# An FFN behind a LoRA projection: scaled f16 parts and seven block products for the base projection of batches 2 and 3

## The reference

```python
base   = x @ W.T                                  # W 1024 x 1024, f32
logits = x @ Wr.T + 5 * onehot(language)          # 8 experts, top 2, softmax -> gates
h_a    = x @ A.T                                  # 8 experts x rank 16 = 128 columns
c      = base + 2 * sum_e gates[e] * (h_a[e] @ B[e].T)
out    = x + (silu(c @ Wg.T) * (c @ Wu.T)) @ Wd.T  # Wg, Wu 3584 x 1024, Wd 1024 x 3584, f16
```

## Time and profile before

| | |
|---|---|
| median of 3 runs | 1346.72 us |
| time of the profiled execution | 1346.81 us |
| its span, first to last instruction | 1345.0 us |
| TensorE clock granted | 1.000 of full speed |
| gate/up of batch 1, of batch 2 | 410.0 to 589.6, 740.0 to 920.1 us of the span |
| route and base of batch 2, of batch 3 | 589.6 to 646.7, 920.2 to 977.2 us |

### The profile page before, as it was taken

The page is one execution under the profiler, slowest core; times in us unless marked ns, Lnnn a source line. Parts: engine busy times, 40 slices in busy tenths (PEclk is TensorE's granted clock), DMA queues, the critical chain, the costliest instruction groups (busy, mean ns, idle before and its releaser), DMA issues.

```text
span 1345.0 us, 20793 instructions
## 1 busy us (share of the span) xinstructions
PE 1339.0 (100%) x8204; PEld 885.9 (66%) x8204; DVE 723.8 (54%) x1335; ACT 387.4 (29%) x626; POOL 173.3 (13%) x159
## 2 busy tenths in 40 slices
PE   9999999999999999999999999999999999999999
PEld 7854444486667666678667666667866766666666
DVE  6478897689524554541542555544173345555612
ACT  4366744352102333322010223332220122222100
POOL 3200112030000132213000113221200011111000
PEclk9999999999999999999999999999999999999999
DMA  7177986225954766502694567650288466666574
GB/s 254 44 262 281 371 294 240 104 98 200 339 181 143 248 215 200 179 27 91 218 332 155 187 218 234 185 161 32 75 277 289 155 178 183 181 189 195 182 231 140
DMA packets 101904, 261.19 MB, mean 194 GB/s; under 512 B 11568, under 2 KB 12208, under 8 KB 101296
## 3 DMA queue, kind: packets, MB, share of 16 engines
q1 hardware_dynamic: 101376, 259.70, 57.6%
q10 hardware_dynamic: 432, 0.17, 0.0%
HBM read 223.91 MB, written 35.91 MB: 193 GB/s over the span
## 4 chain that ended last, share of the span: by engine, by line
PE 97%; DVE 2%; DMA 1%; SPq 0%; issue 0%; ACT 0%; DVEq 0%; ACTq 0%
PE banks L624 22%; PE banks L588 19%; PE banks L645 13%; PE banks L652 13%; PE banks L581 7%; PE banks L580 7%; PE banks L500 4%; PE banks L502 4%; PE banks L501 4%; PE banks L453 1%; DVE h L891 1%; PE banks L676 1%; PE banks L456 1%; DMA a_raw<-AT 0%; PE banks L529 0%; PE banks L527 0%
## 5 line engine op out<-in xcount | busy, mean ns | idle before, releaser
L624 PE MATMUL banks<-y_hi,gu_ring 128*128 128x512 f16 x1344 | 316.5, 379 | 0.0
L624 PEld LDWEIGHTS banks<-y_hi,gu_ring 128*128 128x128 f16 x1344 | 131.5, 98 | 124.0
L645 PE MATMUL banks<-h,piece 128*128 128x512 f16 x840 | 188.5, 379 | 0.0
L580 PE MATMUL banks<-y_hi,gu_ring 128*128 128x512 f16 x432 | 163.7, 379 | 0.0
L581 PE MATMUL banks<-y_lo,gu_ring 128*128 128x512 f16 x432 | 163.7, 379 | 0.0
L1223 ACT ACTIVATE sg<-banks,sc 128x512 f32<-128x512 f32 x112 | 76.7, 686 | 241.1 <-DVE banks L999 131.9
L645 PEld LDWEIGHTS banks<-h,piece 128*128 128x128 f16 x840 | 82.2, 98 | 89.7
L1374 POOL TENSOR_TENSOR m<-m,m 128x256 f32<-128x256 f32 x84 | 61.0, 726 | 528.8 <-DVE m L980 528.8
L1002 DVE TENSOR_TENSOR banks<-banks,m 128x256 f32<-128x256 f32 x84 | 36.4, 433 | 143.7 <-PE banks L624 143.7
L1356 POOL TENSOR_TENSOR w_lo<-w_raw,w_hi 128x1024 fp32r<-128x1024 f32 x31 | 74.9, 2419 | 257.9 <-ACT w_hi L1142 250.0
L652 PE MATMUL banks<-h,piece 128*128 128x256 f16 x896 | 106.1, 273 | 0.0
(11 more groups left out here) (151 smaller groups left out, 1817.4 us busy)
## 6 DMA issues: line engine op xcount, KB each, us to landing
piece<-down_dram SPq DMA_DIRECT2D x80, 448.0 KB, 5.7
mix_c<-mix_dram SPq DMA_DIRECT2D x84, 384.0 KB, 3.9
gu_ring<-Wg SPq DMA_DIRECT2D x112, 256.0 KB, 3.0
gu_ring<-Wu SPq DMA_DIRECT2D x112, 256.0 KB, 2.9
piece<-Wd SPq DMA_DIRECT2D x64, 448.0 KB, 5.7
mix_a<-mix_dram SPq DMA_DIRECT2D x84, 256.0 KB, 2.7
mix_dram<-mixed SPq DMA_DIRECT2D x28, 640.0 KB, 3.8
w_raw<-W SPq DMA_DIRECT2D x32, 512.0 KB, 3.8
```

Source lines behind the costliest of these rows:

```text
L580: MM(bank, w[:, k, :], y_hi[:, k, :], start=(k == 0), stop=False)
L624: mm = MM(bank, w[:, k, :], y_hi[:, k, :], start=False, stop=(k == KC - 1), skip_group_check=True)
L645: mm = MM(bank, w[:, k, :], h[:, half * MH + k, 0, :], start=(start and k == 0), stop=False, skip_group_check=True)
```

## The change

Batches 0 and 1 compute their base as before. For batches 2 and 3:

- x, W, A and Wr are multiplied by a power of two each, from their largest value, and split into an f16 high and an f16 low part. High x high stays 64 matmuls of 512 columns. The two cross products (low x high and high x low), stacked along k, are one product of 2 x 2 blocks, done by seven block products in place of eight: 56 matmuls of 256 columns for a pair of chunks, 224 in a batch. Routing is the same 64 matmuls with f16 operands. LoRA and the transpose stay in f32.
- W's parts and its five block sums are made once, in steps 5 to 25 of batch 1's gate/up, for four pairs of chunks, and written to DRAM (`w16_dram`). For each batch they are loaded back in eight pieces of 256 KB a pair. W's largest value is taken in batch 0's base (`w_max`, eight reductions of 128 x 1024).
- x's largest value, parts and block sums are made on VectorE and ScalarE in steps 7 to 25 of gate/up(1) and gate/up(2). GpSimd makes no more low parts of x and W for these batches.
- In the base each pair of chunks gets the additions of the seven products: two copies on ScalarE, three additions on VectorE, one on GpSimd, and two joins on VectorE (`join`), which write half a chunk of `y_raw` while ScalarE copies the other half. `join(7)` stands behind `h_sums`. `copy_down` of the first pair waits for all eight joins.

The core of the diff (line 1 of a hunk says whose stream it is):

```diff
 # TensorE
+            def fine_route(c, ks):
...
+                for k in ks:
+                    pe.wait_ge(s_xlo, KC * c + k + 1)
+                    for t in range(TT):
+                        at = slice(t * P, (t + 1) * P)
+                        MM(banks[:, t, 0:2 * RC], x16[:, 1, k, at], ar16[:, k].rearrange("p a c -> p (a c)"),
+                           start=(k == 0), stop=False, skip_group_check=True)
+                        mm = MM(banks[:, t, 0:RC], x16[:, 0, k, at], ar16[:, k, 0], start=False,
+                                stop=(k == KC - 1), skip_group_check=True)
...
+            def fine_block(bank, second, w, x, first):
+                at = slice(HALF, T) if second else slice(0, HALF)
+                for a in range(2):
+                    for k in range(KC // 2):
+                        mm = MM(bank[:, at], w[a][:, k, :], x[:, a, k, :], start=(first and a == 0 and k == 0),
+                                stop=False, skip_group_check=True)
...
+            def fine_34(c, p):
+                pe.wait_ge(d_wb[p % 2][1], 48 * wb_loads(c, p))
+                pe.wait_ge(s_bcopy, 2 * (pair_of(c, p) + 1))
...
+            def fine_576(c, p):
+                pe.wait_ge(d_wb[p % 2][2], 48 * wb_loads(c, p))
+                pe.wait_ge(s_bs34, pair_of(c, p) + 1)
...
+            def fine_base(c):
+                fine_route(c, range(0, KC - 2))
+                fine_12(c, 0)
+                fine_route(c, range(KC - 2, KC))
+                fine_34(c, 0)
+                fine_12(c, 1)
+                fine_576(c, 0)
+                fine_34(c, 1)
+                fine_high(c, 0, 0)
+                fine_high(c, 0, 1)
+                fine_576(c, 1)
...
+                fine_576(c, 3)
+                fine_high(c, 3, 0)
+                lora(c, 6)
+                fine_high(c, 3, 1)
+                lora(c, 7)
 # VectorE
+            def w_max(o):
...
+                V.tensor_reduce(w_part[:, o:o + 1], w_hi[:, i, 0].bitcast(F32), AX.XY, ALU.max,
+                                apply_absolute_value=True).then_inc(s_wmx, 1)
...
+            def w_parts(s):
+                if s in W_LOW:
+                    p, row = W_LOW[s]
...
+                    V.scalar_tensor_tensor(out=wp[:, 1, row], in0=wp_raw[:, row], scalar=w_sc[:, 2:3], in1=wp[:, 0, row],
+                                           op0=ALU.mult, op1=ALU.subtract).then_inc(s_wpl, 1)
+                for p, c in W_SUM.get(s, ()):
...
+                    V.tensor_tensor(wp_sum[:, n % 4], left, right, op).then_inc(s_wpsum, 1)
...
+            def join(c, o):
...
+                if o % 2 == 0:
+                    dve.wait_ge(s_b1236, n + 1)
+                    V.tensor_tensor(y_raw[:, o, HALF:T], even_2, m1[:, n % 3], ALU.add).then_inc(s_yfix, 1)
+                else:
+                    dve.wait_ge(s_bs45, n + 1)
+                    V.tensor_tensor(y_raw[:, o, 0:HALF], odd_1, bm45[:, p % 3], ALU.add).then_inc(s_yfix, 1)
...
+                join(c, 6)
+                chunk_max(c, 4)
+                h_sums(c - 1)
+                join(c, 7)
+                chunk_max(c, 5)
+                chunk_max(c, 6)
+                chunk_max(c, 7)
...
             w0_low(1)
             setup()
+            for o in range(W_SLOTS):
+                w_max(o)
             base(0)
...
+                    if b + 1 < NB:
+                        if b == 1:
+                            a_parts(n - MC * b)
+                            w_parts(n - MC * b)
+                        x_parts(b + 1, n - MC * b)
 # ScalarE
             def copy_down(b, q):
                 i = PAIRS * b + q
                 (even, odd), _ = down_banks(q)
+                if q == 0 and FINE <= b + 1 < NB:
+                    act.wait_ge(s_yfix, fixed(b + 1, OC))
 # the steps
+    W_AT = [5 + 5 * p for p in range(OC // 2)]
+    W_LOW = {W_AT[p] + 2 + row: (p, row) for p in range(OC // 2) for row in range(2)}
+    W_SUM = {W_AT[p] + 3 + j: [(p, c) for c in cs] for p in range(OC // 2) for j, cs in enumerate(((0,), (1, 2), (3, 4)))}
+    A_AT = 2
+    X_MAX_AT, X_SCALE_AT, X_SPLIT_AT, X_SUM_AT = 7, 12, 13, 21
```

More of the change, by code:

```diff
@@ L29 @@
 WMAX_FLOOR = 2.0 ** -14
+X_TOP, W_TOP, A_TOP = 13, 13, 14
+TOP_FLOOR = 2.0 ** -40
 GU_SLOTS = 4
@@ new lines, in fine_high @@
+            def fine_high(c, p, row):
+                bank = banks[:, base_bank(c, 2 * p + row), :]
+                if row:
+                    pe.wait_ge(s_bs45, pair_of(c, p) + 1)
+                for k in range(KC):
+                    mm = MM(bank, wb[:, p % 2, HIGH_A if row else HIGH_B, k * 2 // KC, k % (KC // 2), :],
+                            x16[:, 1, k, :], start=False, stop=False, skip_group_check=True)
+                mm.then_inc(s_main, 1)
+            def fine_base(c):
[9 more added lines that the diff above has]
+                fine_576(c, 1)
+                fine_12(c, 2)
+                fine_high(c, 1, 0)
+                turn(c)
+                fine_34(c, 2)
+                fine_high(c, 1, 1)
+                lora(c, 0)
+                lora(c, 1)
+                fine_576(c, 2)
+                lora(c, 2)
+                lora(c, 3)
+                fine_12(c, 3)
+                fine_high(c, 2, 0)
+                lora(c, 4)
+                fine_34(c, 3)
+                fine_high(c, 2, 1)
+                lora(c, 5)
+                fine_576(c, 3)
[3 more added lines that the diff above has]
+                lora(c, 7)
@@ L908, in base @@
                     route(b)
+                if b == 0:
+                    w_max(3)
                 turned_low(b)
@@ new lines, in fine_halves, with fine_cross_34 @@
+            def fine_halves(c, p):
+                even, odd = (banks[:, base_bank(c, 2 * p + row), :] for row in range(2))
+                return even[:, 0:HALF], even[:, HALF:T], odd[:, 0:HALF], odd[:, HALF:T]
+            def fine_cross_34(c, p):
+                even_1, _, _, odd_2 = fine_halves(c, p)
+                n = pair_of(c, p)
+                dve.wait_ge(s_b34, n + 1)
+                dve.wait_ge(s_bcopy, 2 * n + 2)
+                V.tensor_tensor(m32[:, n % 2], odd_2, m32[:, n % 2], ALU.add).then_inc(s_b32, 1)
+                dve.wait_ge(s_b32, n + 1)
+                V.tensor_tensor(bm45[:, p % 3], even_1, m32[:, n % 2], ALU.add).then_inc(s_bs34, 1)
@@ new lines, in fine_copy_12 @@
+            def fine_copy_12(c, p):
+                n = pair_of(c, p)
+                even, odd = (banks[:, base_bank(c, 2 * p + row), 0:HALF] for row in range(2))
+                act.wait_ge(s_b12, n + 1)
+                if p == 0:
+                    act.wait_ge(s_fix, 2 * nth(MC * c - 1))
+                    act.wait_ge(s_1236, nth(MC * c - 1))
+                if n >= 2:
+                    act.wait_ge(s_b1236, n - 1)
+                    act.wait_ge(s_bs34, n - 1)
+                if n >= 3:
+                    act.wait_ge(s_yfix, 2 * n - 5)
+                S.copy(m1[:, n % 3], odd).then_inc(s_bcopy, 1)
+                S.mul(m32[:, n % 2], even, -1.0).then_inc(s_bcopy, 1)
@@ new lines, in copy_half, with fine_base @@
+            def copy_half(c, o):
+                act.wait_ge(s_y, OC * c + o + 1)
+                at = slice(HALF, T) if o % 2 else slice(0, HALF)
+                S.copy(y_raw[:, o, at], banks[:, base_bank(c, o), at]).then_inc(s_yc, 1)
+            def fine_base(c):
+                fine_copy_12(c, 0)
+                route(c)
+                fine_copy_12(c, 1)
+                fine_copy_12(c, 2)
+                turned_high(c)
+                copy_half(c, 0)
+                copy_half(c, 1)
+                copy_half(c, 2)
+                copy_half(c, 3)
+                fine_copy_12(c, 3)
+                for o in range(4, OC):
+                    copy_half(c, o)
```

449 lines of the change are left out of this document (404 added, 45 removed).

## The result

The changed kernel takes 1358.88 us (median of 4 runs, 1358.7 to 1359.09) beside 1346.81 us for the kernel before in the same comparison (1346.48 to 1347.06): a ratio of 1.009, 95% interval 1.0072 to 1.0107. It is 12.1 us slower. The forecast was 1336.5 us, faster, with 1343.0 as the range's upper end.

A forecast was written before the change was run, and what follows sets the result against it. TensorE was taken as the bound, with 97% of the chain. From 1346.8 us, 14.1 saved in two bases less 1.6 of waits in down and 2.2 in gate/up(1) gave 10.3 off: 1336.5, range 1331.5 to 1343.0.

The forecast's parts named there:

- the queue of GpSimd: GpSimd's stream through the change: said to get lighter or stay far from full, with no time booked.
- the four rivals: Waits absent 1332.7 us (0.17); VectorE bounds gate/up(1) 1351 (0.08); late transfers or longer work 1341 (0.15); routing gains nothing 1340 (0.05).
- The new products and the base: TensorE in each base: products fall from 43.6 to 38.2 us, the whole stretch from 57.1 to 50.0 us.
- Routing in f16: Routing before the base: a pair takes 0.18 us instead of 0.235, 1.8 us less a batch, range 0 to 2.0.
- Waits inside the base: Pair 0 of the base: additions and copies come ahead of TensorE, so 0, up to 1 us a batch.
- The wait in down behind join(7): First pair of down: copies come late behind h_sums, TensorE waits 0.8 us, 1.6 for both batches.
- Gate/up(1) and VectorE: Gate/up(1): VectorE gets 46 us of added work; bunching makes TensorE wait 2.2 us in steps 9-12 and 24-27.
- Rival 2: Gate/up(1), steps 7 to 25: VectorE becomes the bound, about 17 us of waits, slower at 1351 us; chance 0.08.
- Transfers: W's traffic in gate/up(1): DMA share about 0.82, step 10's burst fits; 0 booked, up to 4 us.
- Batch 0: Three w_max ahead of batch 0's routing: 3.3 us of delay against 2.4 of slack; 0 booked, bounds 0 and 2.

The follow-up runs named there:

- experiment 1: The changed kernel with the three GpSimd all-reduces of gate/up(1) and (2) replaced by constants, leaving out the maximum across partitions; 1337.43 us.
- experiment 4: experiment 1 with join(7) put ahead of h_sums on VectorE; 1335.72 us.
- experiment 8: experiment 6 with the read two steps behind the store, x's maxima earlier, scales later, and the twelve loads in step 18; 1333.9 us.
- experiment 7: The changed kernel with the twelve loads of W's pieces in batch 2 moved from step 10 to step 18; 1354.74 us.
- experiment 2: The kernel before with three all-reduces of a spare column put into GpSimd's queue, nothing waiting for them; 1356.97 us.
- experiment 6: The changed kernel with maxima across partitions taken by DMA through DRAM and VectorE, W's preparation three steps earlier and join(7) first; 1344.33 us.

## Why the prediction was wrong

**The step that failed** is the queue of GpSimd. The forecast says of it one sentence, "GpSimd and ScalarE get lighter or stay far from full", and books nothing. It counted the instructions that left GpSimd and not the reduces that came, three of them between additions that fall due each step. By busy time the sentence is even true: POOL went from 173.3 us to 125.7, and the three reduces make 1.7 us of that. What they cost isn't busy time. It is the 9.8 to 10.4 us ahead of each and the 7.1 to 8.1 behind it, and they cost 21.5 us of the kernel (experiment 1). None of the four rivals was this one, so the range didn't reach it either.

The trace of before showed the price, in a place of which the forecast makes no use: GpSimd's timeline at W's maximum in batch 0, where nothing waits for it.

```profile
271.14 0.41 POOL L1387 PARTITION_ALL_REDUCE wmax<-wmax  x1 [22.85 <-DVE wmax L874]
279.45 5.19 POOL L1356 TENSOR_TENSOR w_lo<-w_raw,w_hi 128x1024 fp32r<-128x1024 f32 x2 [7.90 <-issue]
```

The 7.90 us behind a 0.41 us reduce, ended by "issue", say that the next tensor operation can't start at once. An addition due each 6.5 us doesn't come through such a change unharmed. The rule was there as well: the Trainium skill ("GPSIMD Engine Reference", section on instruction dispatch) says that the first call of a freshly loaded kernel on GpSimd pays about 6 us more, with no instruction in the profile to show it. The trace agrees for the way into the reduce where the DMA engines aren't full (5.80, 5.93 and 6.06 us); it shows 9.5 to 10.8 where they are, and 7.1 to 9.1 us on the way back, which the page doesn't give. What it does show is the `MODIFY_POOL_CONFIG` at the start of each pause.

**The new products and the base**: right. The bases take 49.9 and 50.0 us, where 50.0 was forecast. The chain of after through the base of batch 3:

```profile
944.34 0.12 PE banks L666
944.52 0.12 PE banks L666
...
945.74 7.86 PE banks L701 x72
953.60 3.45 PE banks L753 x16
```

Block products are 7.86/72 = 0.109 us and high products 3.45/16 = 0.216, as priced from the earlier trace rows.

**Routing in f16**: right, and at its lower bound. The pair is 0.175 us (944.34 to 944.52, with the seven pairs from there to 945.74 at the same step; 0.18 was taken), so the term is bound by its columns. **Waits inside the base**: none, as said.

**The wait in down behind join(7)**: right. Two waits of 1.6 us together in after, where 0.8 each was forecast, and 1.7 us come back when the join is put first (experiment 4). The chain of after shows the order that was stepped through, `join(7)` after `h_sums`, then the second copy, then the products:

```profile
999.96 0.43 DVE y_raw L1376
...
1000.68 0.38 ACT d L1855
...
1001.11 1.70 PE banks L945 x14
```

**Gate/up(1) and VectorE**: right in mechanism and nearly in size. The groups of the added work, by form, answer to the rates taken from the earlier trace rows (busy us, mean ns of one, idle before):

```profile
L1305 DVE TENSOR_TENSOR wp_sum<-wp 128x1024 f16<-128x1024 f16 x20 | 13.1, 686 | 0.1
L1295 DVE SCALAR_TENSOR_TENSOR wp<-wp_raw,w_sc,wp 128x1024 f16<-128x1024 f32 x8 | 10.2, 1278 | 0.0
L1338 DVE TENSOR_TENSOR xs<-x 128x2048 f16<-128x2048 f16 x8 | 9.8, 1219 | 0.0
```

Forecast were 13 us, 10.2 and 1.2 each. Of waits 2.2 us were forecast; experiment 1 is 3.0 above before in that stage, and spreading the work gives 1.8 back. Rival 2, the slower case, put a loss in this stage too, at 1351. It was not what happened: with VectorE's work untouched, experiment 1 runs at 1337.4. Nor do VectorE and GpSimd visibly hold each other up, as that rival had it: a sum of W takes 686 ns where the nearest row had 692, and GpSimd's addition 724 ns in after and 726 before.

**Transfers**: right as to the weights. In gate/up(1) the share is 0.84 in experiment 8 (0.82 was forecast) and no product waits for a weight. But they weren't free for others: the burst in step 10 of batch 2, booked at 0, made the third reduce 4 us longer and cost 7.2 us through it (experiment 7). **Batch 0**: right, `down(0)` starts at 315.2 us after 315.6 before, with the three `w_max` in it. They take 3.5 us; the forecast set 3.3 against the slack, though its own 1.3 us each make 3.9.

The forecast without the reduces, 1336.5, stands 0.9 us from experiment 1 at 1337.4. One missing term made 21.5 of the 22.4 us of error. That the rest is so small is in part luck, for smaller misses went both ways: by experiment 1's stages the bases gained 14.6 us and not 14.1, but the two stages with gate/up lost 4.3 us where 3.0 were forecast. The later expectations missed as well, and at the same place: for experiment 2 each reduce was charged 7 to 8 us, where only the part of the gap beyond what the schedule covers is paid; and for experiment 6 the small store was taken to be done within a step of 6.5 us and took 9 to 12.

## What to carry to other kernels

Go through every queue for what a change puts into it, not only for what it takes out, and price an instruction by the distance between its neighbours and not by its busy time; look for the same operation elsewhere in the trace and read the idle time behind it. An engine that is busy 9% of the span can still make the span longer, if another kind of work is put between operations that fall due each step. Where a value across partitions is needed beside such a stream, it can go another way than through GpSimd, if the way has two steps' room.

## What the runs showed of the hardware

- A `partition_all_reduce` of one column takes 0.41 us on GpSimd (0.76 to 0.90 in three places), and 13.4 to 19.1 us go from the addition before it to the addition after it. Busy time shows none of it. Directly behind another reduce there is no such pause (67.02 us in after).
- The way into it is 5.8 to 6.1 us at a DMA share of 0.66 to 0.81 and 9.5 to 10.8 at 0.97 or more; the way out, in the twelve places in gate/up, is 7.1 to 9.1.
- After a stop of 4 to 6 us TensorE was granted 1.2 GHz for the next 3 to 5 us: about 2 us more for each stop.
- With a store of 128 partitions by 4 bytes in a queue of large transfers, 9 to 12 us went from its issue to the issue of the read that waits for it (experiment 6); the load of 128 copies of a row of 512 bytes landed in 3.6 to 8.7.
